# Masked cross attention: one maximum product per step, and the first expert weights loaded and split ahead of the norm

## The reference

```
x = x + L0_xattn(norm(x), ctx)         one head of width 128
x = x + L0_attn(norm(x))               16 heads of 8, causal over 64
x = x + L0_ffn(norm(x))                8 gated experts of 512, top 2, written densely
x = x + L1_xattn(norm(x), ctx, mask)   16 heads of 8 over 1601 keys, then self attention and FFN
x = x + L1_attn(norm(x))               16 heads, fake quantised to 8 bits
x = x + L1_ffn(norm(x))                8 experts of 512, top 2
```

```
q, k, v = split(x @ qw + qb), split(ctx @ kw + kb), split(ctx @ vw + vb)
probs = softmax(q . k / sqrt(8) + mask)         16 heads, 64 queries, 1601 keys
out   = probs . v
```

## Time and profile before

| | us |
|---|---|
| median of 3 runs | 1376.42 |
| lowest and highest | 1372.77, 1376.95 |
| the profiled execution: time | 1376.45 |
| its span | 1374.6 |
| PE busy | 1044.6 (76%) |
| DVE busy | 724.5 (53%) |
| ACT busy | 489.2 (36%) |
| POOL busy | 223.0 (16%) |

### The profile page before, as it was taken

The page is one execution under the profiler, slowest core; times in us unless marked ns, Lnnn a source line. Parts: engine busy times, 40 slices in busy tenths (PEclk is TensorE's granted clock), DMA queues, the critical chain, the costliest instruction groups (busy, mean ns, idle before and its releaser), DMA issues.

```text
span 1374.6 us, 22315 instructions
## 1 busy us (share of the span) xinstructions
PE 1044.6 (76%) x9246; PEld 738.4 (54%) x9246; DVE 724.5 (53%) x1194; ACT 489.2 (36%) x633; POOL 223.0 (16%) x202
## 2 busy tenths in 40 slices
PE   3676774998863789999999999998476545729888
PEld 1455453777751356666666666665345323428766
DVE  4234766433443556666666656663376477864121
ACT  0235231222231145555555555555223102403333
POOL 2000423121221001111111111100142004220110
PEclk9899886999995589999999999999888867758999
DMA  8581010010302332222333233320000000010110
GB/s 264 193 342 76 1 43 4 25 45 23 93 0 91 112 117 102 101 100 101 115 132 125 100 109 115 103 73 17 1 1 0 1 0 0 1 31 16 32 37 24
DMA packets 41346, 98.47 MB, mean 72 GB/s; under 512 B 9976, under 2 KB 24960, under 8 KB 41264
## 3 DMA queue, kind: packets, MB, share of 16 engines
q1 hardware_dynamic: 41264, 97.29, 20.9%
HBM read 55.49 MB, written 0.73 MB: 41 GB/s over the span
## 4 chain that ended last, share of the span: by engine, by line
PE 46%; DVE 17%; issue 15%; ACT 11%; POOL 4%; SPq 3%; DMA 3%; DVEq 0%; POOLq 0%
PE PS L262 44%; ACT PT L1084 7%; DVE kl L1475 3%; DVE mx L1492 3%; ACT kh L1071 2%; DVE prT L1481 2%; SPq L893 2%; DVE u_all L275 1%; POOL work_area L390 1%; DMA ctxT<-in_ctx_T 1%; POOL PT L390 1%; DVE x L675 1%; POOL blank_g L257 1%; POOL rstd_all L281 1%; PE PS L292 1%
## 5 line engine op out<-in xcount | busy, mean ns | idle before, releaser
L1492 DVE TENSOR_REDUCE mx<-PS 128x2 f32<-128x1024 f32 x192 | 230.4, 1217 | 74.8 <-PE PS L262 74.6
L1084 ACT ACTIVATE PT<-PS 128x1024 f32<-128x1024 f32 (+1 forms) x208 | 212.4, 1021 | 97.9 <-PE PS L262 97.9
L262 PE MATMUL PS<-QB,KS 128*128 128x256 f32 (+1 forms) x832 | 166.8, 323 | 25.1 <-ACT PT L1084 17.9
L262 PE MATMUL PS<-QB,QS 128*128 128x512 f32 x576 | 159.1, 425 | 24.5 <-DVE wcol L663 22.5
L262 PEld LDWEIGHTS PS<-QB,KS 128*128 128x128 f32 (+1 forms) x832 | 115.7, 187 | 70.2 <-ACT PT L1084 37.6
L262 PEld LDWEIGHTS PS<-QB,QS 128*128 128x128 f32 x576 | 109.7, 201 | 61.5 <-issue 27.6
L262 PE MATMUL PS<-PT,work_area 128*32 128x128 f32 (+1 forms) x3328 | 134.4, 279 | 0.5 <-ACT PT L1084 0.5
L262 PE MATMUL PS<-KS,QB 64*128 64x512 f32 (+1 forms) x512 | 109.7, 459 | 11.5 <-DMA KS<-kl 9.5
L675 DVE SCALAR_TENSOR_TENSOR x<-PS,wcol,x 128x128 f32<-128x128 f32 x128 | 44.9, 350 | 138.1 <-PE PS L262 134.7
L262 PEld LDWEIGHTS PS<-PT,work_area 128*32 128x32 f32 (+1 forms) x3328 | 78.4, 109 | 43.6 <-issue 36.2
L262 PE MATMUL PS<-nat_area,work_area 128*128 128x128 f32 (+2 forms) x928 | 85.0, 275 | 13.7 <-DVE work_area L670 5.9
(11 more groups left out here) (240 smaller groups left out, 1420.1 us busy)
## 6 DMA issues: line engine op xcount, KB each, us to landing
KS<-kh SPq DMA_DIRECT2D x32, 800.5 KB
ctxT<-in_ctx_T SPq DMA_DIRECT2D x24, 800.5 KB, 4.9
nat_area<-in_ctx_tiles SPq DMA_DIRECT2D x16, 832.0 KB, 6.5
KS<-kl SPq DMA_DIRECT2D x16, 800.5 KB
work_area<-in_ctx_T SPq DMA_DIRECT2D x8, 800.5 KB, 10.1
nat_area<-in_L_ffn_experts_w SPq DMA_DIRECT2D x24, 256.0 KB, 3.2
nat_area<-in_L_ffn_W SPq DMA_DIRECT2D x16, 256.0 KB, 3.0
KS<-mask_parts SPq DMA_DIRECT2D x32, 50.1 KB
```

The lines of the kernel that those rows point to most:

```text
L262: return T.matmul(o, l, r, start=start, stop=stop, **k)
L1084: P["exp_a"].done(S.activation(PT[0:rows, par, :], PS[0:rows, 1024:2048], ACT.Exp), f"e{k}")
L1492: ins = V.reduce_max(by_pair[:, :, j // 3, j % 3:j % 3 + 1], src, AX)
```

## The change

Nothing is computed differently. In the masked cross attention every step gets one maximum product: 3 to 12 in steps 0 to 9, and 0 to 2 of the next batch in steps 10 to 12. Keys move one step ahead, to steps 0 to 3; the sum to step 4; the 13 value tiles are no longer made in four bursts but two per step in steps 5 to 8, four in step 9, and the last in step 11, with nm between, in step 10. TensorE does the side work of a step before the value product instead of behind it, and nm before the maximum. ScalarE copies the sums into SBUF, and VectorE takes the reciprocal there. `V_all` moves out of `expert_area`; so SyncE can load the first experts earlier, and GpSimd splits them before the power of the norm.

```
-        V_all = expert_area[:, 0:2 * TOKENS]
+        V_all = early[:, 512:512 + 2 * TOKENS]
...
-            b = n + 1 if k < 11 else n + 2
-            return [(b, j) for j in MAX_STEPS[k]] if 0 <= b < BATCH else []
+            b, j = (n + 1, k + 3) if k < 10 else (n + 2, k - 10)
+            return [(b, j)] if 0 <= b < BATCH else []
...
+        def sides(n, k):
+            return [item for item in SIDES[k]
+                    if 0 <= n + (1 if isinstance(item, int) else SIDE_OF[item[0]]) < BATCH]
+        def closed(items):
+            out = []
+            for item in items:
+                if not isinstance(item, int):
+                    out.append(item)
+                elif item + 1 == sum(TG[value_group(item)]):
+                    out.append(f"v{value_group(item)}")
+            return out
...
-            heads_done(sp, "a0")
+            at(sp, "cc_p", "pc", PAIRS - 1)
             moe_sync(sp, "e0", (A["L0_ffn_experts_w1"], A["L0_ffn_experts_w3"], A["L0_ffn_experts_w2"], None))
...
-            heads_done(sp, "a2")
+            heads_done(sp, "a1")
             moe_sync(sp, "e1", (A["L1_ffn_W1"], None, A["L1_ffn_W2"], A["L1_ffn_b1"]))
...
             attn_gpsimd("a0")
+            moe_gpsimd("e0", True, 0)
             ln_all_gpsimd(2)
-            with g.Fori(0, EXPERTS // 2) as i:
-                moe_gpsimd("e0", True, i)
+            with g.Fori(0, EXPERTS // 2 - 1) as i:
+                moe_gpsimd("e0", True, i + 1)
...
             attn_gpsimd("a2")
+            moe_gpsimd("e1", False, 0)
             all_max(4, "O", "qx_v")
...
+                if item[0] == "s":
+                    at(S, "sum_p", item, n - 1)
+                    if n >= 2:
+                        at(S, "fin_g", "on", n - 2)
+                    P["sum_a"].done(S.activation(rsum, bank(7, 256), ACT.Copy), item)
...
-                    for b, j in maxima(n, k)[:1]:
+                    items = sides(n, k)
+                    if "nm" in items:
+                        beside("nm", n, k)
+                    for b, j in maxima(n, k):
                         maximum(b, j)
+                    for item in items:
+                        if item != "nm":
+                            beside(item, n, k)
                     if k and 0 <= n < BATCH:
                         values(n, k - 1)
                     if k == 0 and n >= 1:
                         values(n - 1, KT - 1)
-                    for b, j in maxima(n, k)[1:]:
-                        maximum(b, j)
-                    if side(n, k):
-                        beside(k, n)
...
-                    at(V, "sum_p", "sum", n - 1)
-                    if n >= 2:
-                        at(V, "fin_g", "on", n - 2)
-                    P["sum_v"].done(V.reciprocal(rsum, bank(7, 256)), "sum")
+                    at(V, "sum_a", "sum", n - 1)
+                    P["sum_v"].done(V.reciprocal(rsum, rsum), "sum")
...
-MAX_STEPS = ([2], [3], [4], [5], [6], [7, 8], [9], [10, 11], [12], [], [], [0], [1])
-SIDES = (None, "k0", "k1", "k2", "k3", "sum", "v0", "v1", "v2", "v3", "nm", None, None)
+SIDES = (("k0",), ("k1",), ("k2",), ("k3",), ("sum",), (0, 1), (2, 3), (4, 5), (6, 7), (8, 9, 10, 11), ("nm",), (12,), ())
```

More of the change, by code:

```diff
@@ L740, in build @@
         progress("sum_p", ["sum"])
+        progress("sum_a", ["sum"])
         progress("sum_v", ["sum"])
@@ L805, in maxima, with value_group, bank7_free @@
         def maxima(n, k):
-            b = n + 1 if k < 11 else n + 2
-            return [(b, j) for j in MAX_STEPS[k]] if 0 <= b < BATCH else []
+            b, j = (n + 1, k + 3) if k < 10 else (n + 2, k - 10)
+            return [(b, j)] if 0 <= b < BATCH else []
         SIDE_OF = {"k": 2, "v": 1, "n": 1, "s": -1}
[L812 to L819, removed]
+        def value_group(c):
+            return next(g for g, (k0, k) in enumerate(TG) if k0 <= c < k0 + k)
+        def sides(n, k):
[9 more added lines that the diff above has]
+            return out
+        def bank7_free(n, k):
+            before = [(m, item) for m in range(-2, n + 1) for i in range(KT) for item in closed(sides(m, i))
+                      if (m, i) < (n, k)]
             if before:
-                m, i = before[-1]
-                item = SIDES[i]
+                m, item = before[-1]
                 b = m + SIDE_OF[item[0]]
                 if item == "sum":
-                    at(nc.tensor, "sum_v", "sum", b)
+                    at(nc.tensor, "sum_a", "sum", b)
                 elif item[0] == "v":
@@ L1004, in _ @@
             ln_all_gpsimd(8)
-            with g.Fori(0, EXPERTS // 2) as i:
-                moe_gpsimd("e1", False, i)
+            with g.Fori(0, EXPERTS // 2 - 1) as i:
+                moe_gpsimd("e1", False, i + 1)
         @block.scalar
@@ L1089, in slot @@
                         P["acc_a"].done(S.activation(acc_sb, bank(6, 256), ACT.Copy), "acc")
-                    if side(n, k):
-                        empty(SIDES[k], n)
+                    for item in closed(sides(n, k)):
+                        empty(item, n)
             slots(slot)
@@ L1209, in _, with beside @@
                 P["q3_p"].done(mm(bank(h), W["L1_xattn_cq_w"][:, :], xT_all[:, 512 * h:512 * h + 512]), f"q{h}")
-            def beside(k, n):
-                item = SIDES[k]
-                bank7_free(k, n)
+            def beside(item, n, k):
                 if item == "sum":
+                    bank7_free(n, k)
                     at(T, "acc_a", "acc", n - 1)
                     P["sum_p"].done(mm(bank(7, 256), consts[:, C_SEL:C_SEL + 128], acc_sb), "sum")
[L1218 to L1226, removed]
+                elif item == "nm":
+                    bank7_free(n, k)
+                    at(T, "max_v", "nm", n + 1)
+                    P["max_p"].done(T.transpose(bank(7, 128, 8), nm[:, :], ident), "nm")
+                elif isinstance(item, int):
+                    g = value_group(item)
+                    k0, count = TG[g]
+                    if item == k0:
+                        bank7_free(n, k)
+                    rows = 128 if item < FULL else TAIL
+                    o = 3584 + 128 * (item - k0)
+                    last = mm(PS[0:rows, o:o + 128], ctxT[:, (n + 1) % 2, 128 * item:128 * item + rows], W["L1_xattn_cv_w"][:, :])
+                    if item + 1 == k0 + count:
+                        P["vals_p"].done(last, f"v{g}")
+                else:
+                    bank7_free(n, k)
                     c0, cw = CHUNKS[int(item[1])]
@@ L1232, in beside @@
                     P["keys_p"].done(mm(bank(7, cw), W["L1_xattn_ck_w"][:, :], ctxT[:, n % 2, c0:c0 + cw]), item)
-                else:
-                    at(T, "max_v", "nm", n + 1)
-                    P["max_p"].done(T.transpose(bank(7, 128, 8), nm[:, :], ident), "nm")
             def maximum(b, j):
@@ L1501, in slot @@
                 for k in range(KT):
+                    items = closed(sides(n, k))
+                    if "nm" in items:
+                        beside("nm", n)
                     for b, j in maxima(n, k):
                         maximum(b, j)
-                    if side(n, k):
-                        beside(SIDES[k], n)
+                    for item in items:
+                        if item[0] in "ks":
+                            beside(item, n)
             ln_all_vector(3, x, u_all)
```

1 line of the change is left out of this document (removed).

## The result

The change takes 1436.9 us (median; 1434.07 to 1438.1), against 1376.56 for the kernel before: a ratio of 1.0442, 95% interval 1.0418 to 1.0466. I had forecast 1375, with a range up to 1389. It is **slower** by 60 us, and outside the range (1351 to 1389). The profiled executions differ by 61.2 us in span (1435.8 against 1374.6).

What follows compares the result with a forecast made beforehand. A masked cross attention slot was taken as bound by TensorE, unevenly across steps. From 1376.45 us, +3.3 (slots with the wait), -8.7 (norms) and +3.9 (clock) gave 1374.95, forecast 1375 us, range 1351 to 1389.

Steps and rivals of the forecast that it cites:

- The norms, -10.9 + 2.2: Ahead of both expert blocks, normalising operations fall to 2.14 us, saving 10.9; contention with splits costs 2.2; net -8.7 us.
- The contention in the attentions' tails: VectorE subtractions and GpSimd splits hold each other up while attention's last tiles finish: 0 to 4.2 us, taken as 2.2.
- The wait in step 0: Masked cross attention, slots 1 to 13: scores wait 2.2 us for nml, queued on SP behind the next context's load.
- no wait at all: Rival: masked cross attention slots shorten as walked, without waiting for nml, 13 x -1.67 = -21.7 us: 1342; chance 5%.
- the small transfer does not wait: Rival: nml need not wait for the big load, slot wait 0.75 us, no clock falls: 1352 us; chance 13%.
- The walk, 29.46: Masked cross attention slot summed step by step without the wait: 29.46 us, 1.67 less than the kernel before.
- The steps that I had at 2.12: Steps 5 to 8 of a masked cross attention slot: 0.65 + 0.43 + 0.46 + 0.58 = 2.12 us each.
- the one at 2.65: Step 9 of a masked cross attention slot, with four value tiles and the last maximum: 2.65 us.
- the first key interval: Start of a masked cross attention slot: copy acc delays kh, so the interval is about 3.4 us instead of 2.68.
- The clock, +3.9: Slots 1 to 13: TensorE's clock falls to half after 3 of 13 waits, 1.3 us each: +3.9 us.
- clock falls after nearly every wait: Rival: in slots 1 to 13 the clock falls 13 times instead of 3, at 1.3 us: 1388 us; chance 17%.

Runs made afterwards that it cites:

- the second part alone: Kernel before with only V_all moved, first experts loaded earlier and their splits ahead of the norm: 1367.16 us, ratio 0.992.
- the run with idle products: The change plus 1152 columns of products without use on TensorE during step 0's wait for nml in slots 1 to 13: 1401.46 us, ratio 1.016.
- the last run: The change with the last value tile moved forward and the value product ahead of the side work in each step: 1333.48 us, ratio 0.9674.
- another run: The change plus 512 columns of products without use at the start of step 0's wait in slots 1 to 13: 1405.04 us.
- the run without the queueing: The change with SyncE issuing nmh and nml ahead of the load of the next context: 1379.36 us, ratio 1.001.

## Why the prediction was wrong

Going through its own steps:

- **The norms, -10.9 + 2.2**: right in the durations, 2.14 us in both blocks, and the total of 8.7 lies in the interval of the second part alone. The gain of the first block is shown (6 to 7 us), that of the second only in the mean of the runs (some 4 us; 1.7 in the change). The contention in the attentions' tails (0.8 us each in the change, by the same markers) is within what these stages vary between runs, so its size is not shown.
- **The wait in step 0**: right in place, cause and count (SyncE's order, slots 1 to 13), and nearly in size: 2.4 us, not 2.2, some 3 us in all. I also looked only at who waits for nml: the first key product waits for the load itself. Without that, two of my rivals looked better than they were. With the tile in step 11, "no wait at all" (1342) would have lost another 0.98 us in each of 13 slots, and "the small transfer does not wait" (1352) what its own wait of 0.75 left of it.
- **The walk, 29.46**: wrong in its premise on the order, "the side work stands ahead of the value product", which I priced at the acc copy in step 0 alone. With the value product first (and the last tile early) the slot is 28.98, half a microsecond better than the walk. As the change orders it, 31.27. The steps that I had at 2.12 took 2.31, the one at 2.65 took 2.77 to 2.89, and the first key interval 3.57 instead of 3.4. I took the products' distances from the earlier trace rows, where each stands next to a given neighbour, and kept them for other neighbours; two tiles between a maximum and a value product are not half of four ahead of scores. It is 1.8 us a slot, 23 us. Slot 14 came to 27.5 instead of 26.2.
- **The clock, +3.9**: wrong in count and in price, and the largest miss. I expected 3 falls of 13 at 1.3 us; there were 13 of 13 at 2.9, some 37 us. The one row that I had for a fall lasted 3.4 us, and I took that for its length; seven of the thirteen lasted three times as long. The rival "clock falls after nearly every wait" named the mechanism, at under half its price.

Together: 0.2 (wait) + 1.8 (walk) + 2.6 (clock) = 4.6 us a slot, 60 us in 13 slots, and the miss is 61.9.

Read as a ladder, each rung a run, in us per slot: 31.13 before; -2.15 for the even arrangement with the value product first (1.08 of it the copy of the sums, 0.89 one maximum a step); +2.29 for the order within the step; +0.98 for the late tile by its own data; +1.44 for nml behind the load; +2.88 for the clock; 36.57. The last two use the nine slots of the run with idle products in which nml was not late; with all twelve they are 1.76 and 2.56.

## What to carry to other kernels

When a change reorders work on TensorE, the neighbours of a product have a price, not only the product: measure each in the order that it will have, and try work of one weight shape side by side. When a load is made to wait for later work, look at everything behind it in its queue and at every reader of its data. A standstill of TensorE within a busy stretch has two prices, its own length and the low clock behind it, and the second can be the larger; where the wait can't go, products without use can buy the clock back.

## What the runs showed of the hardware that I had not expected

- After standstills of 2.2 to 2.7 us the granted clock stayed at 1.2 GHz for 3.4, 6.8 or 10.2 us with TensorE busy. In the slot shown it fell at 655.0, a microsecond before the scores started. With the standstill filled down to 0.1 to 0.4 us, in three slots 1.5 to 1.7, it stayed at 2.4 GHz in all of these slots. One standstill of 1.17 us, in slot 1 of the last run, was followed by 6.8 us of low clock, where eleven of 0.86 to 1.57 us in another run were not.
- The order of the same products within a step changed the time by 0.2 us per step. Eight value tiles took 1.09 us up to a value product and 0.92 up to scores.
- 4 KB queued behind an 800 KB load was usable 4.75 us after that load's issue and 3.6 us after its own; in the run without the queueing the load itself was usable 4.28 us after its issue. So the small transfer came some 0.5 us behind the large one. At some starts, with no change in the program's order, it came a further 1.3 us later.
